# Layer one of a four-layer graph network: the rectifier moves to VectorE, one-hot matrices are built in two halves, and ScalarE fetches eight tiles of rows by itself

## The reference

```
pe  = relu(edge_w @ pos_w1) @ pos_w2      # edge_w: two numbers of each edge
x_j = x[src]                              # 50000 rows gathered from 3125
msg = pe * x_j + x_j
s   = segment_sum(msg, dst);  agg = s / max(cnt, 1)
out = relu(batchnorm(concat([x, agg]) @ sage_w + sage_b)) + x
```

## Time and profile before

| what | us |
|---|---|
| median of 3 runs | 4296.28 (4295.04 to 4298.53) |
| the profiled execution's own time | 4292.06 |
| its span, first to last instruction | 4290.2 |
| first gather of layer one starts | 2238.46 |
| last gather of layer one starts | 2733.12 |
| last message of layer one starts | 2747.24 |
| sums of layer one are copied out from | 2749.66 |

### The profile page before, as it was taken

One profiled execution on the slowest core, in us unless ns is written; L12 is line 12 of the kernel. 1 busy time (PEld: TensorE's weight loads), 2 busy tenths in 40 slices (PEclk: granted clock), 3 DMA queues, 4 the chain that ended last, 5 costly groups with the idle time before them and its releaser, 6 DMA issues. The chain is left out here.

```text
span 4290.2 us, 67945 instructions
## 1 busy us (share of the span) xinstructions
PE 2843.9 (66%) x12192; PEld 2150.4 (50%) x12193; DVE 1800.1 (42%) x4747; ACT 432.5 (10%) x703; POOL 2729.0 (64%) x2866
## 2 busy tenths in 40 slices
PE   7556585555855568666677777775557756654697
PEld 3444444444444444444447666644445556654574
DVE  4222252222522226344463333422223666667874
ACT  2000020000200002000021111210000111111334
POOL 2777767777677776777737777367775377774000
PEclk9776797777977779777889999967777888887799
DMA  5222222222222222222212222122221255543340
GB/s 156 56 55 56 55 89 56 55 55 55 89 55 56 55 55 88 56 55 55 60 53 54 54 54 54 27 56 55 55 56 43 68 154 157 157 153 106 109 146 15
DMA packets 167914, 315.15 MB, mean 73 GB/s; under 512 B 63863, under 2 KB 89662, under 8 KB 167138
## 3 DMA queue, kind: packets, MB, share of 16 engines
q0 software_dynamic: 94528, 207.40, 19.9%
q1 hardware_dynamic: 62882, 102.69, 7.7%
q10 hardware_dynamic: 10240, 2.64, 0.7%
HBM read 250.84 MB, written 61.65 MB: 73 GB/s over the span
## 5 line engine op out<-in xcount | busy, mean ns | idle before, releaser
L690 POOL DMA_INDIRECT ring<-m_tab,idx x1536 | 1459.1, 950 | 557.0 <-issue 464.0
L1637 PE MATMUL ps<-oh,ring 128*128 128x256 f32 (+1 forms) x2902 | 910.7, 477 | 511.2 <-DMA ring<-m_tab,idx 413.6
L1637 PE MATMUL ps<-nodes,ring 128*128 128x256 f32 (+1 forms) x2766 | 828.5, 461 | 427.2 <-DMA ring<-m_tab,idx 319.2
L1637 PEld LDWEIGHTS ps<-oh,ring 128*128 128x128 f32 x2902 | 656.6, 249 | 656.1 <-issue 551.8
L1637 PEld LDWEIGHTS ps<-nodes,ring 128*128 128x128 f32 x2766 | 604.0, 241 | 562.4 <-issue 467.0
L690 POOL DMA_INDIRECT ring<-x_tab,idx x768 | 729.1, 949 | 244.2 <-issue 228.5
L1151 DVE TENSOR_SCALAR oh<-iota,dl 128x256 f32<-128x256 f32 x1248 | 382.3, 377 | 980.3 <-PE ps L1637 963.1
L1151 DVE TENSOR_SCALAR nodes<-iota,dl 128x256 f32<-128x256 f32 x1175 | 364.7, 380 | 749.5 <-PE ps L1637 749.5
L690 POOL DMA_INDIRECT ring<-kv_tab,idx x416 | 402.3, 967 | 149.1 <-issue 126.4
L710 POOL TENSOR_TENSOR small<-small,bc 128x4 f32<-128x4 f32 (+1 forms) x28 | 31.0, 1108 | 458.6 <-DVE small L1248 458.6
L1637 PE MATMUL ps<-wpad,rts 128*128 128x128 f32 x832 | 159.2, 369 | 177.3 <-DVE pw L1414 177.3
(11 more groups left out here) (257 smaller groups left out, 2541.2 us busy)
## 6 DMA issues: line engine op xcount, KB each, us to landing
ring<-m_tab SPq DMA_DIRECT2D x4096, 0.5 KB
ring<-m_tab ACTq DMA_DIRECT2D x4096, 0.5 KB
ring<-x_tab SPq DMA_DIRECT2D x2048, 0.5 KB
ve_dr<-pw SPq DMA_DIRECT2D x52, 512.0 KB, 3.0
ring<-ve_dr SPq DMA_DIRECT2D x52, 512.0 KB, 3.4
ring<-m_tab,idx POOLq DMA_INDIRECT x1548, 3.0
m_tab<-ring SPq DMA_DIRECT2D x75, 256.0 KB, 2.2
ring<-x_tab ACTq DMA_DIRECT2D x1024, 0.5 KB
```

What stands on the lines that cost most here:

```text
L690: pool.indirect_dma_start(rows[:, j, :], None, table, bass.IndirectOffsetOnAxis(ap=idx[:, wave * WV + j:wave * WV + j + 1], axis=0)).then_ ...
L1637: return T.matmul(o, lhsT, rhs, start=start, stop=stop, skip_group_check=True)
```

## The change

- `relus` on ScalarE is gone. VectorE rectifies the half itself, with a `tensor_scalar` (max with 0) from PSUM into `pw`, as the first thing of each half.
- VectorE copies `rts` of the next wave in the first half (after the rectifier) and builds the one-hot matrices 0 to 3 of the next wave there, and 4 to 7 in the second half. The wait on `credit` stays in the second half.
- ScalarE runs `act_rows(act, x_tab[0], xrow)` at the start of layer one: 1024 row DMAs for wave 49. Its wait for the row numbers (`xi_ld`, 64) moves from layer two to here. GpSimd's eight gathers at L696 go, with the semaphore `x_l1`; 387 remain.
- In `L1_POS` wave 49 (FULL + 1) is processed one place later, behind wave 45.

```diff
-        L1_POS = (FULL - 8, ..., FULL, FULL - 4, FULL + 1, FULL - 3, FULL - 2, FULL - 1, FULL + 2)
-        L1_THEN_ACT = FULL - 4
+        L1_POS = (FULL - 8, ..., FULL, FULL - 4, FULL - 3, FULL + 1, FULL - 2, FULL - 1, FULL + 2)
...
-                    if k == PASS_L1 and g == L1_THEN_ACT:
-                        for t in range(SP_TILES, SP_TILES + ACT_TILES):
-                            pool.indirect_dma_start(far_slot(t), None, table, ...).then_inc(x_l1, 16)
...
-            def relus(i, waves):
-                for u, wave in enumerate(waves):
-                    for hf in halves(wave):
-                        q = (i * DEPTH + u) * 2 + hf
-                        act.wait_ge(l1_hid, q + 1)
-                        nc.scalar.activation(pw[:, hf, :], ps[:, 7, :], ACT.Relu).then_inc(l1_relu, 1)
-            whole_turns(act, relus)
+            act.wait_ge(xi_ld, 64)
+            for c in range(2):
+                act.wait_ge(ln_dma[c], LN_DMA(1, c))
+            act_rows(act, x_tab[0], xrow)
             evac(PASS_L1)
...
+                    ahead = waves[u + 1] if u + 1 < len(waves) else i * DEPTH + (u + 1)
                     for hf in halves(wave):
-                        if hf:
-                            ahead = waves[u + 1] if u + 1 < len(waves) else i * DEPTH + (u + 1)
-                            dve.wait_ge(credit, wave_no(PASS_L1, i, u) + DEPTH)
-                            V.tensor_scalar(rts[:, (u + 1) % 2, :], recT[:, ds(ahead * P, P)], 0.0, None, ALU.add)
-                            pair_hot(u + 1, ahead, WV).then_inc(oh_ready, 1)
+                        q = (i * DEPTH + u) * 2 + hf
+                        dve.wait_ge(l1_hid, q + 1)
+                        V.tensor_scalar(pw[:, hf, :], ps[:, 7, :], 0.0, None, ALU.max).then_inc(l1_relu, 1)
+                        if len(halves(wave)) == 2:
+                            if hf:
+                                dve.wait_ge(credit, wave_no(PASS_L1, i, u) + DEPTH)
+                            else:
+                                V.tensor_scalar(rts[:, (u + 1) % 2, :], recT[:, ds(ahead * P, P)], 0.0, None, ALU.add)
+                            ins = pair_hot(u + 1, ahead, WV // 2, hf * (WV // 2))
+                            if hf:
+                                ins.then_inc(oh_ready, 1)
                         arrived(dve, PASS_L1, i, u, wave)
```

More of the change, by code:

```diff
@@ L309, in build @@
         x_pl = sem("x_pl")
-        x_l1 = sem("x_l1")
         s_wpad = sem("s_wpad")
@@ L401, in build @@
         LAST_POS = (FULL - 4, FULL - 3, FULL, FULL - 2, FULL + 1, FULL + 2, FULL - 1)
-        L1_POS = (FULL - 8, FULL - 7, FULL - 6, FULL - 5, FULL, FULL - 4, FULL + 1, FULL - 3, FULL - 2, FULL - 1, FULL + 2)
-        L1_THEN_ACT = FULL - 4
+        L1_POS = (FULL - 8, FULL - 7, FULL - 6, FULL - 5, FULL, FULL - 4, FULL - 3, FULL + 1, FULL - 2, FULL - 1, FULL + 2)
         def tiles_of(wave):
@@ L456, in act_rows @@
             far_rows(act, mybir.EngineType.Activation, table, at[1], SP_TILES, ACT_TILES, x_ac)
-        def after_l1(k):
-            return isinstance(k, int) and k >= PASS_L1
         def far_landed(eng, k):
-            by_act = k if after_l1(k) else k + 1
             eng.wait_ge(x_pl, (k + 1) * (16 * POOL_FAR))
@@ L467, in far_landed @@
                 eng.wait_ge(x_sp[b], (k + 1) * X_SP)
-                eng.wait_ge(x_ac[b], by_act * X_AC)
+                eng.wait_ge(x_ac[b], (k + 1) * X_AC)
         def far_arrived(eng, k, wave):
@@ L476, in far_arrived @@
                 eng.wait_ge(x_pl, (k + 1) * (16 * POOL_FAR))
-            elif isinstance(k, int) and k == PASS_L1:
-                eng.wait_ge(x_l1, 16 * ACT_TILES)
             else:
                 for b in range(4):
-                    eng.wait_ge(x_ac[b], (k if after_l1(k) else k + 1) * X_AC)
+                    eng.wait_ge(x_ac[b], (k + 1) * X_AC)
         def arrived(eng, k, i, u, wave):
@@ L693, in gathers @@
                         ).then_inc(gat_end if slots == NEAR and g == FULL - 1 and j >= LAST_SPLIT else gat[u], 16)
-                    if k == PASS_L1 and g == L1_THEN_ACT:
-                        for t in range(SP_TILES, SP_TILES + ACT_TILES):
-                            pool.indirect_dma_start(
-                                far_slot(t), None, table,
-                                bass.IndirectOffsetOnAxis(ap=idx[:, NEAR + t:NEAR + t + 1], axis=0)).then_inc(x_l1, 16)
                     if slots == NEAR and g == (FULL - 1 if k == PASS_L1 else LOOPED * DEPTH - 1):
@@ L873, in _ @@
             hidden(STEPS, "L2")
-            act.wait_ge(xi_ld, 64)
             for c in range(2):
@@ L1146, in _, with pair_hot @@
                     step(f"{L}_b{n}", V.tensor_tensor(b_(f"{L}_b{n}"), b_(f"{L}_bih_{n}"), b_(f"{L}_bhh_{n}"), ALU.add))
-            def pair_hot(u, wave, n):
-                for j in range(n):
+            def pair_hot(u, wave, n, first=0):
+                for j in range(first, first + n):
                     ins = V.tensor_scalar(pair_oh(u, j), iota2[:, :], dl2[:, ds(wave * WV + j, 1)], None, ALU.is_equal)
@@ L1324, in messages @@
                             all_arrived(dve, PASS_L1)
-                        dve.wait_ge(l1_pe, (i * DEPTH + u) * 2 + (hf + 1))
+                        dve.wait_ge(l1_pe, q + 1)
                         xj = wave_rows(wave, u)[:, 4 * hf:4 * hf + 4, :]
```

## The result

| | before | after |
|---|---|---|
| median of 13 runs each, us | 4293.06 | 4306.94 |
| ratio, with its 95% interval | | 1.0033 (1.0026 to 1.0040) |
| span of the profiled execution, us | 4290.2 | 4307.1 |

The change costs 14 us; 11.4 were forecast. The page of the changed kernel shows where the work went: ScalarE lost 60 us, VectorE gained 67, GpSimd issued eight instructions less, and the queue q10 (ScalarE's) has 12288 packets instead of 10240.

A forecast was written before the change was run, and what follows sets the result against it. Layer one's loop waits for gather landings, its end for TensorE's last 14 half waves. Four terms of 0, -1 for GpSimd's pace and +12.4 for later landings give +11.4: 4296.28 to 4307.7 us, range 4298 to 4314.

The forecast's parts named there:

- The landings: Layer one's gathers, with both row streams running, land after 14 to 16 us from wave 24, growing before, instead of 2.5.
- Wave 43: Its first message in layer one goes from 2681.87 to 2694.3, +12.4 us on the path.
- The tail: After wave 43's first message, 14 half waves of TensorE at 4.67 us each stay as before.
- GpSimd: Eight gathers fewer behind wave 44's: 10.0 us less on GpSimd, 0 on the path.
- The pace term: Gathers up to wave 43 meet VectorE's matrix building less often: -1 us, bounds -2 and +3.
- The rectifier: On VectorE at each half's start: takes 0.69 us, done at +2.63 at the latest, hidden, 0 on the path.
- Short landings: Rival: layer one's landings stay at 2.5 us and nothing changes, 4295 to 4296 us; 10%.
- The number of gathers: Rival: GpSimd's gather count sets layer one's end, 10 us gained, 4286 us; 4%.
- A throttled GpSimd: Rival: delay above some 23 us holds GpSimd for slots over the last 20 waves, 12 us more, 4319; 4%.
- VectorE late in each half: Rival: late by 0.3 us per tail half wave, 4 us on top, 4311; counted within the main case's range.

The follow-up runs named there:

- g2_no_rows_387: g1_vector_part with 387 gathers and the new wave order, nobody fetching wave 49 in layer one (stale rows); ratio 0.9991 to the kernel before.
- g3_scalar_stream_alone: Changed kernel without SyncE's row fetches in layer one, ScalarE's 1024 row DMAs the only stream; ratio 0.9991 to the kernel before.
- g1_vector_part: Kernel before with only VectorE's rectifier and one-hot halves, 395 gathers, no ScalarE rows in layer one; 4287.25 us beside 4292.00, ratio 0.9988.
- f4_half_stream: Changed kernel with ScalarE fetching only four tiles of wave 49 (512 row DMAs), GpSimd gathering the other four; ratio 1.0008 to the kernel before.

## Why the prediction was right

**The landings.** Forecast: 14 to 16 us after wave 24, growing before. Measured, from a wave's last gather to its first message: 4.3 us at wave 0, 7.8 at wave 6, 13.2 at wave 16, 16.2 at wave 23, and then 15.3 to 16.5 but for waves 24 to 27 (up to 18.2) and 41 (17.2), where TensorE was late. Layer two of the same trace was a good model of a stage that did not exist yet. g2_no_rows_387 and g3_scalar_stream_alone show the cause that the prediction had inferred from one difference between stages. One of its readings does not carry what it was used for: the line of landing times in the earlier trace rows covers only a few transfers, most of them near the layer's end. The changed kernel's own line reads like this, beside its two streams:

```profile
L445 ACTq DMA_DIRECT2D ring<-x_tab x1024: 213/214/537, 2241.3 to 2679.7; - x171
...
L445 SPq DMA_DIRECT2D ring<-x_tab x1024: 227/228/586, 2245.0 to 2681.6; - x171
...
DMA to landing us min/median/max: 2.3/2.6/3.7
```

The 2.5 us of layer one before stands all the same, by the chain and by the first messages that waited for a landing.

**Wave 43.** Forecast: its first message 455.8 us after the first gather (2694.3 - 2238.46) less 1 for GpSimd; measured 455.85. A detail was off: I let wave 41 be the last landing that TensorE waits for and wave 43's fall. It was wave 43's own, 16.06 us (the row of the chain in the first section), since the streams ran until 2680 and 2682 and its last gather started at 2680.25. ScalarE's ended 7 us later than forecast, 2 of them because the layer began later. The message came 1.0 us later than the 454.8 that this sum gives with the -1, so the detail cost little.

**The tail.** Forecast: 14 half waves as before. Measured: 2761.76 - 2696.33 = 65.43 us, before 65.37.

**GpSimd.** Forecast: 10 us less and none of it on the path. Measured: the last gather 10.97 us earlier, and the layer 12.5 later. The pace term, -1 for fewer meetings with VectorE, measured -1.18 up to wave 43. Its size is right and its reason is not: the forecast took it from landings that drift, but g1_vector_part, with landings of 2.5 us, has wave 43's last gather 439.86 us after the first, -1.09. It comes with VectorE's part.

**The rectifier.** Forecast 0.69 us, hidden. It takes 0.69 in each of 101, where ScalarE took 0.60, and TensorE waited for it 11 times, 8.6 us in all, as it did for ScalarE (11 times, 7.6 us).

```profile
L1301 DVE TENSOR_SCALAR pw<-ps x101: 691/692/693, 2245.9 to 2759.1; 128x512 f32<-128x512 f32 x101
...
  PE ps L1625: 8.6, 11
```

The Trainium skill ("VectorE: DVE Perf Modes", the TRN2 errata) gave an estimate of 0.66 us; the trace has 0.692, and by either it stays hidden.

**What the size missed.** 13.9 us by the medians against 11.4. In the stage it is 12.5 against 11.4, and that difference is wave 43's landing. The other 1.4 us lie within the interval of the ratio, 11 to 17 us. The time itself, 4307.7 forecast and 4306.94 measured, is closer than it deserves, and that is luck: the median of three runs that it started from was 3.2 us too high, and the change 2.5 us too low.

**The rivals.** Short landings: against it stands the landing of 16.06 us in the chain. The number of gathers: against g2_no_rows_387. A throttled GpSimd: its last gather came 11 us early, so it was not held; the delay stayed at 16. VectorE late in each half: TensorE waited for its rectifier 11 times, as for ScalarE's before, and the tail's halves are as long as before.

## What to carry to other kernels

An engine that has the most busy time may be off the path for the last part of its stage: count what the other side still has to do after the last arrival that it waits for, before work is taken from the first. That the DMA engines are mostly idle does not make a fetch free that is moved to another queue; look at what the same queues do to each other in another stage of the same trace. And a delay that is over is not yet paid: the consumer makes it up only at the difference of the two paces, so a far wave belongs where the consumer has slack, and the delay before it must be small.

## What the runs showed of the hardware that was not expected

- In the runs of 4283 to 4307 us, one stream of 512-byte row DMAs at 0.40 to 0.41 us each leaves the indirect gathers (128 rows of 512 bytes, one every 1.25 us) at 2.5 us to landing, whichever of the two engines issues it. Both streams together, at 0.43 us each, let the landing grow by about 0.6 us for each eight gathers, to 16 us, and no further, while the DMA engines are busy 27% of the time. Why it grows and why it stops at 16 us was not tried. The 27% is a mean over 16 engines and cannot show whether one of them is full. The queue of the gathers, from 2500 to 2600 us, in the changed kernel and in g3_scalar_stream_alone:

```profile
q0 software_dynamic: 2559, 5.25, 24.7%
...
q0 software_dynamic: 2542, 5.24, 19.8%
```

  The same packets take a quarter more time, and it is not spread over all: in the packet records of the traces 68 of the 1280 packets of 4096 bytes in these 100 us took more than 0.7 us with both streams. In the kernel before, in g1_vector_part, g2_no_rows_387 and g3_scalar_stream_alone, and in f4_half_stream, whose second stream had ended, none took more than 0.54. That is near one packet in 16 and would fit one overloaded engine of the 16; the records do not name the engine, so this is not shown.
- That one stream is harmless does not hold everywhere: in the runs of some 6500 us, at 0.54 to 0.59 us for each row DMA, the first message of wave 20 came 44 to 45 us after its last gather with one stream alone.
- TensorE fell to the lower clock (1.2 GHz) for part of single half waves when it had stood idle for a while: in the changed kernel a half took 6.3 us instead of 4.63 seven times. In the one at wave 6, after 2.5 us without work, the granted clock was 0.54 from 2320 to 2323 us. Over whole stretches it was below full speed in the two before wave 24, where it was 1.00 before.

```profile
2300.00:2400.00 100.00, 75.74 (x459) 66.94 (x459) 49.86 (x124) 0.00 (x0) 75.59 (x81) 0.97 0.28 55
2400.00:2500.00 100.00, 75.69 (x449) 66.77 (x448) 49.04 (x122) 0.00 (x0) 75.56 (x81) 0.95 0.27 55
```

  Each costs 1.7 us. All seven came before wave 43, whose first message still waited for its landing, so none of them moved the end.
- With the rectifier on VectorE a half wave in the loop takes 4.63 us instead of 4.56 in the seven profiles of these runs that have it, with one stream or two: VectorE's message starts 0.11 us after TensorE's last product instead of 0.04. What this is was not looked into.
